# Six PSUM banks for the selected columns of a two-layer graph network, the other users of PSUM on two

## The reference, cut to what matters

```
# layer 0
ew   = (edge_attr_16 @ W_e + b_e).reshape(E, 16, 16)
msg  = einsum('ei,eio->eo', x[src], ew)
x    = layernorm(x + segment_sum(msg, dst) / max(count, 1) + bias)
# layer 1
msg  = einsum('emh,eh->em', edge_emb[edge_type_8].reshape(-1, 16, 16), x[src])
m    = segment_sum(msg, dst)
x    = layernorm(x + GRU(m, x; w_ih, w_hh, b_ih, b_hh))
```

## Time and profile before

| what | value |
|---|---|
| three runs, median | 6261.09 us (6250.47 to 6273.0) |
| span of the profiled execution | 6277.1 us (its own time outside the profiler is not given) |
| TensorE busy | 5108.7 us (81%) |
| VectorE busy | 3968.6 us (63%) |
| ScalarE busy | 4007.9 us (64%) |
| GpSimd busy | 3566.7 us (57%) |
| mean granted TensorE clock | 0.921 |

### The profile page before, as it was taken

How to read it: one execution, slowest core, us unless ns; L and a number is a source line. 1 busy time by engine, 2 the same in 40 slices (tenths; PEclk the granted TensorE clock), 3 DMA queues, 4 the chain that set the end, 5 groups by cost and what they waited for, 6 DMA issues and landing times.

```text
span 6277.1 us, 131101 instructions
## 1 busy us (share of the span) xinstructions
PE 5108.7 (81%) x39898; PEld 4605.9 (73%) x39899; DVE 3968.6 (63%) x4891; ACT 4007.9 (64%) x5658; POOL 3566.7 (57%) x3745
## 2 busy tenths in 40 slices
PE   6888888888888888888777877778887778877777
PEld 5777777777777777777577777777777777777777
DVE  6666666676666666666655555555555555555556
ACT  6666666666666666666556666666666666666665
POOL 6555555555555555555555555555555555555554
PEclk9999999999999999999889989899999888988998
DMA  3111111111111111111111111111111111111110
GB/s 63 27 29 28 28 29 28 29 27 30 27 29 27 28 29 28 29 27 28 21 21 22 20 21 20 20 20 21 21 21 21 20 20 22 20 21 20 21 21 14
DMA packets 336894, 156.46 MB, mean 25 GB/s; under 512 B 196220, under 2 KB 335963, under 8 KB 336723
## 3 DMA queue, kind: packets, MB, share of 16 engines
q1 hardware_dynamic: 218224, 124.50, 8.9%
q0 software_dynamic: 118464, 30.56, 7.0%
q10 hardware_dynamic: 160, 0.80, 0.1%
HBM read 152.87 MB, written 2.66 MB: 25 GB/s over the span
## 4 chain that ended last, share of the span: by engine, by line
PE 54%; issue 15%; ACT 14%; another core or an unknown queue 12%; DVE 4%; ACTq 1%; DVEq 0%; POOL 0%; DMA 0%; SPq 0%; POOLq 0%
PE psN L782 43%; PE psM L819 9%; ACT dist L576 7%; ACT pick L584 6%; DVE cand L982 1%; DVE z L1013 1%; ACTq L329 1%; PE psTR L800 1%; DVE z L988 0%; ACT sumT L560 0%; ACT psD L599 0%; PE psTR L790 0%; PE psTR L803 0%; ACTq L575 0%
## 5 line engine op out<-in xcount | busy, mean ns | idle before, releaser
L782 PE MATMUL psN<-table_hi,pick 128*128 128x320 f32 x12740 | 4038.1, 332 | 919.2 <-ACT pick L584 538.2
L782 PE MATMUL psN<-table_lo,pick 128*128 128x320 f32 x12740 | 3909.2, 321 | 13.8 <-issue 13.0
L782 PEld LDWEIGHTS psN<-table_hi,pick 128*128 128x128 f32 x12740 | 2575.5, 202 | 1125.4 <-ACT pick L584 585.0
L782 PEld LDWEIGHTS psN<-table_lo,pick 128*128 128x128 f32 x12740 | 2579.4, 202 | 19.0 <-issue 17.8
L504 POOL DMA_INDIRECT z<-h_rows,idx x1817 | 1737.9, 956 | 1379.2 <-PE psN L782 619.9
L504 POOL DMA_INDIRECT z<-in_x,idx x1885 | 1802.4, 956 | 1264.3 <-issue 496.3
L982 DVE TENSOR_TENSOR cand<-psN,grp_hot 128x640 f32<-128x640 f32 (+1 forms) x1306 | 1043.8, 805 | 1964.7 <-PE psN L782 1273.2
L584 ACT ACTIVATE pick<-dist,one 128x640 fp32r<-128x640 bf16 (+1 forms) x2485 | 1978.6, 835 | 412.3 <-remote 248.0
L576 ACT ACTIVATE dist<-src_mod,neg_node 128x640 bf16<-128x640 uint16 (+1 forms) x2485 | 1970.5, 831 | 33.0 <-ACT pick L584 15.7
L1013 DVE TENSOR_TENSOR z<-psD,z 128x2048 f32<-128x2048 f32 (+1 forms) x750 | 1366.9, 1823 | 55.0 <-issue 33.2
L603 ACT COPY sumS<-psM 128x273 f32<-128x273 f32 (+1 forms) x250 | 81.9, 328 | 1697.4 <-PE psM L819 1258.5
(11 more groups left out here) (109 smaller groups left out, 759.4 us busy)
## 6 DMA issues: line engine op xcount, KB each, us to landing
src_mod<-src_mod_rows SPq DMA_DIRECT2D x434, 160.0 KB
z<-in_x,idx POOLq DMA_INDIRECT x1885
z<-h_rows,idx POOLq DMA_INDIRECT x1817
eab<-in_edge_attr SPq DMA_DIRECT2D x125, 200.0 KB
src_mod<-src_mod_rows SPq DMA_DIRECT2D x63, 192.0 KB
idx<-in_src SPq DMA_DIRECT2D x250, 12.5 KB
dstb<-in_dst SPq DMA_DIRECT2D x250, 14.0 KB
grp<-src_grp SPq DMA_DIRECT2D x249, 5.5 KB
```

Of the source, the lines that this page charges most:

```text
L782: mm = pe.matmul(rows[:, :, 0:cells.shape[2]], pick[j][:, c, at:at + P], cells, start=(i == 0 and part == 0), stop=(i == TC - 1 and part = ...
```

## The change

`psN` gets six banks in place of four. The block's sum, its transposes and its result share one bank (psM), coefficients and relative destinations another (psD). In layer 0 there is one buffer of coefficients instead of two, and VectorE writes it in `match_block`, not ScalarE. Since the sum of a block now goes into the bank that the result of the block before was read from, TensorE waits on `acc` before `sum_block`. In the loop for further windows the wait on `acc` goes ahead of the sum too; the page counts 12500 records of the sum's matmul, which is 50 for each of the 250 blocks, so this loop's body never runs. `TURN` of layer 0 becomes 12. The buffer `cand` in SBUF keeps its four places (`N_CAND`).

```
-TURN = (10, 12)
-RING = 4
+RING = 6
+TURN = (12, 12)
+N_CAND = 4
...
-        cand = sb("cand", [P, RING, F, NG])
+        cand = sb("cand", [P, N_CAND, F, NG])
...
-        psTR = ps("psTR", [P, PB])
-        psT, psR = psTR[:, 0:3 * P], psTR[:, 3 * P:4 * P]
+        psT, psR = psM[:, 0:3 * P], psM[:, 3 * P:4 * P]
         psN = ps("psN", [P, RING, PB])
-        psD = [ps(f"psD{b}", [P, PB]) for b in range(2)]
-        coef = [[m[:, 0:G * F].rearrange("p (g n) -> p g n", n=F) for m in psD],
-                [psD[0][:, b * G * T:(b + 1) * G * T].rearrange("p (g n) -> p g n", n=T) for b in range(2)]]
-        rel = [psD[1 - b][:, PB - GPAD:PB] for b in range(2)]
+        psD = ps("psD", [P, PB])
+        coef = [[psD[:, 0:G * F].rearrange("p (g n) -> p g n", n=F)] * 2,
+                [psD[:, b * G * T:(b + 1) * G * T].rearrange("p (g n) -> p g n", n=T) for b in range(2)]]
+        rel = [psD[:, PB - (b + 1) * GPAD:PB - b * GPAD] for b in range(2)]
...
-                def copy_coef(b, buf, r):
-                    act.wait_ge(l["inp"][buf], 32 * (r + 1))
-                    act.wait_ge(l["z"], NS * b)
-                    act.wait_ge(l["match"], b)
-                    act.copy(coef[0][buf], eab[buf][:]).then_inc(l["coef"], 1)
...
                         if t == S_AT[k]:
+                            pe.wait_ge(l["acc"], SUB * b + 1)
                             pe.wait_ge(l["match"], b + 1)
...
+                def coefficients(b, buf):
+                    dve.wait_ge(l["z"], NS * (b + 1))
+                    dve.tensor_copy(coef[0][buf], eab[buf][:]).then_inc(l["coef"], 1)
+
                 def match_block(b, buf, r):
                     relative(b, buf, r)
-                    if k == 1:
+                    if k == 0:
+                        if not (isinstance(b, int) and b == 0):
+                            coefficients(b, buf)
+                    else:
```

More of the change, by code:

```diff
@@ L180, in build @@
         psM = ps("psM", [P, PB])
-        psTR = ps("psTR", [P, PB])
-        psT, psR = psTR[:, 0:3 * P], psTR[:, 3 * P:4 * P]
+        psT, psR = psM[:, 0:3 * P], psM[:, 3 * P:4 * P]
         psN = ps("psN", [P, RING, PB])
-        psD = [ps(f"psD{b}", [P, PB]) for b in range(2)]
-        coef = [[m[:, 0:G * F].rearrange("p (g n) -> p g n", n=F) for m in psD],
-                [psD[0][:, b * G * T:(b + 1) * G * T].rearrange("p (g n) -> p g n", n=T) for b in range(2)]]
-        rel = [psD[1 - b][:, PB - GPAD:PB] for b in range(2)]
-        assert G * F <= PB - GPAD
+        psD = ps("psD", [P, PB])
+        coef = [[psD[:, 0:G * F].rearrange("p (g n) -> p g n", n=F)] * 2,
+                [psD[:, b * G * T:(b + 1) * G * T].rearrange("p (g n) -> p g n", n=T) for b in range(2)]]
+        rel = [psD[:, PB - (b + 1) * GPAD:PB - b * GPAD] for b in range(2)]
+        assert ZW <= 3 * P and max(G * F, 2 * G * T) <= PB - 2 * GPAD
         s_w = sem("s_w")
@@ L622, in begin @@
                     if k == 0:
-                        copy_coef(0, 0, 0)
                         whole_half(1, 1, 0, 0)
@@ L632, in first_body @@
                     if k == 0:
-                        copy_coef(1, 1, 0)
                         act.wait_ge(s_meta, 1)
@@ L638, in first_body @@
                     first_rows(0)
-                    if k == 0:
-                        copy_coef(2, 0, 1)
                     sums_of_windows(n_win)
@@ L656, in body @@
                         first_rows(b)
-                        if more2:
-                            copy_coef(b + 2, buf, r + 1)
                     else:
@@ L833, in window @@
                     def window(x, q):
+                        pe.wait_ge(l["acc"], SUB * b + SUB + 1)
                         pe.wait_ge(l["match_x"], x + 1)
@@ L836, in window @@
                         pe.wait_ge(l["mS_x"], x + 1)
-                        pe.wait_ge(l["acc"], SUB * b + SUB + 1)
                         pe.wait_ge(l["acc_x"], SUB * x + 1)
@@ L1049, in first_body @@
                         group_hot(1, 1, 0)
+                        dve.wait_ge(l["inp"][0], 32)
+                        coefficients(0, 0)
                         outer(0, 0, 0, 0)
```

## The result

The changed kernel takes 6214.6 us (median of 4 runs, 6201.0 to 6231.5) where the kernel before takes 6255.8 us beside it (4 runs, 6242.8 to 6273.0). The ratio is 0.9934, 95% interval 0.9905 to 0.9962: 41 us, 0.66% faster. A second measurement of the same pair on a chip of that kind gave 0.9927 (0.9905 to 0.9949). The forecast was 6180 us, with a range of 6070 to 6330. The profiled execution took 6231.5 us, its span 6229.7 us.

The account below looks back on a forecast made before the run. No engine is full; a loop of waits through several engines, with late turn signals, sets the time. Layer 1's 53 us plus layer 0's 28, all else 0, make 81 us: 6261 - 81 = 6180 us, range 6070 to 6330.

Parts of the forecast that it names:

- Direction and place: Layer 1: turns 0 and 1 move ahead of a select, idle time moves before the sum; faster by more than 0.3%: 0.56.
- The late signal: A turn's signal to VectorE can come nearly 5 us behind the turn; more banks don't bring it sooner.
- Layer 1, the start of the sum: At full clock, gains of 1.88 us behind ten turns and 0.16 behind eleven, mean 1.02 us a block.
- 0.3 us for the signal: Layer 1: ScalarE's copy starts 0.61 us behind the sum; half, 0.3 us a block, taken as gained, bounds 0 and 0.61.
- the share of slow sums: Layer 1: 40% of sums at full clock, 60% slow at half clock, after 3.8 us of idle time.
- the forecast's own formula: Layer 1: 0.4 x (1.02 + 0.3) - 0.6 x (0.46 - 0.3) = 0.43 us a block, 53 us gained.
- The rival of the clock: Clock falls at layer 1's sum and the turn behind it; at 80% slow sums 47 us lost, 6308 us; chance 0.25.
- Layer 0: Turn 4 needn't wait for the select of turns 0 and 1; 110.5 us of waits halved twice, 28 us gained.
- Copies and banks: VectorE's 125 coefficient copies of 0.5 us are covered by its waits; shared banks and the wait on acc cost 0.
- Nothing moves: Rival: late signals and the gathers pacing them set the period, TensorE's work between is free; 6261 us; chance 0.15.
- all sums fast: Rival: every sum of layer 1 runs at full clock; 192 us gained, 6069 us; chance 0.13.
- VectorE becomes the bound: Rival, in layer 0: 63 to 122 us of copies on VectorE make it the bound; 6243 to 6302 us; chance 0.05.

Follow-up runs that it names:

- the runs with four banks: Changed kernel with RING = 4 and TURN = (10, 12), shared banks and VectorE copies kept, against the kernel before, second kind of chip: ratios 0.9995 and 0.9993.
- the second copy: Changed kernel with VectorE also copying layer 0's coefficients to a scratch tile each block, against the kernel before, second kind of chip: 4846.8 us, ratio 0.9815.
- the kernel with the later sum: Changed kernel with layer 1's sum behind turn 2, not turn 1, and transposes behind turn 4, first kind of chip: 6113.0 us, ratio 0.9753 against the kernel before.

## Why the prediction was right, and what was mis-sized

**Direction and place: right.** The late signal stays (4.91 us idle ahead of a select after, 4.47 before); six banks only let TensorE go on meanwhile. In layer 1 turns 0 and 1 no longer stand before a bank (86 us for the whole layer, 558 before), and the idle time stands ahead of the sum, released by the outer piece. This is the most certain part: it shows in all three profiles with six banks in layer 1 and the sum behind turn 1.

**Layer 1, the start of the sum: right in size, not in the split.** I worked out 1.02 us earlier and 0.3 us for the signal, 1.32 together. By the records from 3150 to 6050 us a sum started 21.77 us (behind eleven turns) and 23.31 us (behind ten) after the end of the one before it, and starts 20.96 and 21.40 us after it now: 0.81 and 1.91 us earlier, in the mean 1.36. With the signal the forecast had 0.46 and 2.18. That the mean comes so near is partly luck: the second profile of the changed kernel against six banks in layer 0 alone, on one chip, gives 0.87 and 1.52, in the mean 1.19. Nor is the 0.3 us for the signal shown by itself. And the measure counts from the end of the last sum; it says what the block gained only if the block pays for all of a longer sum.

**Does it pay?** These three profiles speak for it, without proving it. The time from one sum's start to the next grows with the first one's length, by 1.00 us for each us (give or take 0.07) behind ten turns and by 0.87 (0.22) behind eleven. But that rests on sums with long stops inside them; among those without a stop it is 0.12 (0.59) and 0.99 (0.35), which settles nothing.

**Layer 1, the share of slow sums: the term that was mis-sized.** "I take 40% of the sums at full clock, 60% slow, since 3.8 us is a bit nearer to 4.79 than to 2.96." It was 19% and 81% (23 and 96 of 119). What made it wrong was reading 3.8 us as a middle between 2.96 and 4.79: in these profiles 187 of the 188 sums behind 3.8 us or more of idle time spent over 1 us at the lower level, 52 of 56 behind 3.4 to 3.8, and 13 of 43 behind 3.0 to 3.4. The mean sum went from 2.22 to 3.24 us, 1.02 us longer where 0.89 was allowed for (0.6 x 1.48). With the measured share the forecast's own formula gives 0.19 x 1.32 - 0.81 x 0.16 = 0.12 us, 15 us instead of 53; timed by layer it was 22 us (11 to 32). The nearness of 15 to 22 confirms little, as that formula leaves out the slower turn behind the sum (next paragraph), and the records' own sum, 1.36 - 1.02 = 0.34 us a block or 42 us, is the profiled executions' gain and not the timed one. The Trainium skill ("TensorE: Matmul & The Clock Gate", section "Why this matters for your kernels") asks for short gaps between bursts of matmuls; the trace agrees, with 0.50 granted behind 4.00 us of idle time.

**The rival of the clock: its mechanism came, its sign did not.** It put the point from which slow sums eat the gain at 61%, and 80% at a loss. The share passed that, and the kernel is still faster. The rival charged 0.55 us for turn 2, half of the 1.1 us by which a window of 4 us was to outlast the sum. That was a slip, for 4.0 - 3.20 is 0.8 and its half 0.4. By the records the first turn behind a sum ended 0.33 us later than before (2.06 us behind the sum against 1.73), in most blocks with one slow matmul and then starts at the full-clock spacing. And the rival left out the 0.3 us of the signal. With both put right its sum at 81% is 124 x (0.19 x 1.32 - 0.81 x 0.49) = -18 us in layer 1, +28 in layer 0, 10 us gained in place of 47 lost, and still 31 us short of the measurement. It is not shown what gave these back.

**Layer 0: right.** 28 us forecast, 23 us timed (12 to 34). The halving of 110 us twice had no row behind it, so the nearness is luck in part. A cost that the forecast didn't have is in it: the stops inside the sum of layer 0 came to 17 and 40 us (150 to 3080 us) in the two profiles with four banks in that layer on the first kind, and to 75 to 80 in the four with six. On the second kind, where with four banks the wait of turn 4 is the only one in layer 0, the ring is worth more: 0.84 us a block.

**Copies and banks: right.** 0 forecast; 0.01% by the sum of layers on the first kind, give or take 0.3%, and 0.9995 and 0.9993 on the second with four banks. A copy takes 0.57 us, not 0.5. With six banks on the second kind a second one isn't quite free: 0.08 us a block. No wait on `acc` shows at the sum of layer 1: 113 of 119 start with the outer piece's end.

**The sum.** 81 us forecast, 41 to 44 measured. 31 of the missing us are layer 1's, where the share of slow sums is worth 38 by the formula, though by the records the sums are only 0.13 us longer than allowed for, 16 us; 5 are layer 0's and within its interval.

**"Nothing moves" and "all sums fast" are out**, by the intervals of both measurements and by the median of 421 ns. "VectorE becomes the bound" is out on the second kind by the runs with four banks and with the second copy, and on the first by layer 0's own gain.

## What to carry to other kernels

A deeper ring of banks moves a wait, and what it is worth is what the next wait leaves: here TensorE's idle time went from ahead of two turns to ahead of the sum, which then ran at half clock, and of 1.36 us by which it starts earlier 1.02 went into its own length. If a change opens a gap of some 4 us in front of matmuls that lie on the path, try to put other matmuls there: one turn moved into it was worth 103 us on one chip, against 41 to 44 for the banks, while on another chip it cost 65 us with four banks. And time a split by layer rather than read it off two profiles: 0.2 us a block was 23 us of real time and not to be seen in single executions. Where TensorE has no idle time left, as in layer 0 on the second kind, a deeper ring has given all that it can. Before keeping such an order of work, run it on a second chip.

## What the runs showed of the hardware

**The same kernel takes 6256 to 6260 us on one kind of chip and 4939 us on two others.** The number of instructions and the work are the same; the page with four banks on a chip of the second kind:
```profile
PE 4650.6 (94%) x39898; PEld 4282.0 (87%) x39899; DVE 4004.1 (81%) x5016; ACT 3946.8 (80%) x5533; POOL 3598.7 (73%) x3745
```
Against the changed kernel on the first kind VectorE, ScalarE and GpSimd are busy the same time within 1%, TensorE 432 us less, at a clock of 1.00 in both layers instead of 0.96 and 0.90. What differs is the waiting. VectorE's select for the turns of layer 0, with four banks on the second kind (150 to 2450 us, 116 blocks, at most 0.8 us):
```profile
DVE cand L971 <- PE psN L770: 177.2, 233, 0.8
DVE cand L971 <- issue: 33.1, 117, 0.3
```
and in the kernel before on the first kind (150 to 3080 us, 120 blocks, up to 8.0 us):
```profile
DVE cand L982 <- PE psN L782: 555.3, 271, 8.0
DVE cand L982 <- remote: 232.9, 55, 4.5
```
So the signals that the forecast took for a property of the kernel are late, nearly throughout, on one kind of chip only.

**TensorE stops for up to 1.8 us inside a run of matmuls, on the first kind only.** The stops of 0.95 and 0.43 us within turn 1 in the timeline of the result wait for nothing that the profile shows. In the sums of layer 1 of the kernel with the later sum such stops come to 0.80 us a sum (3150 to 6050 us); on the second kind, with four banks, there are none in 117 sums (2600 to 4800 us). They fall at nearly the same place of the program each time: in the sums of one parity most of them ahead of matmul 24 to 27 of the 50 (counted from 0), in those of the other most often ahead of 13 to 15. In other kernels of the first kind the places differ: after the change most of them lie ahead of matmul 43 in the sums of one parity. A fixed place makes one think of the supply of instructions. The Trainium skill ("Runtime: NRT & Kernel Launch", section "Instruction fetch mechanics") has the instruction memory of an engine refilled in blocks of 16 KiB as the program runs, and the trace agrees as far as that it has 27 transfers of 16,384 bytes of the kind "instruction". But in the kernel with the later sum there is no transfer of that kind between 3227 and 6023 us, nearly the whole stretch in which the stops were counted, and in every other profile too they lie around the starts and ends of the two loops alone. So refills from memory, as far as the trace records them, are not the cause. What stops TensorE, and whether it also delays the signals, is open.
